# Expert blocks of a two-layer transformer kernel: pairs finished one by one, high terms of the down projection first, weight casts placed around

## The chip, the cores and the metric

The kernel runs on one core of a Trainium2 chip. The metric is the device time of one execution in microseconds; the median of three runs of the kernel before is 967.14 us (966.48 to 967.25). The core has five engines with their own instruction streams: TensorE (matmuls, PE), VectorE (DVE), ScalarE (ACT), GpSimd (POOL) and SyncE (SP, which here only starts transfers). Each engine works through its stream in order and waits on semaphores.

## The reference, cut to what matters

Two layers, each attention and then a mixture of experts, over 2048 tokens of width 256. The change touches the experts alone.

```python
# layer 0: 8 experts, inner width 1024, two per token
hidden = silu(x_flat @ wge.T) * (x_flat @ wue.T)
acc = acc + we[:, None] * (hidden @ wde.T)
# layer 1: 8 experts, inner width 512, two per token, at most 640 rows each
h = einsum('ecd,edf->ecf', exp_batches, W1); inp, gate = split(h, 2, axis=-1)
h = gelu(inp, approximate=False) * gate
exp_out = einsum('eci,eid->ecd', h, W2)
```

## The kernel before, in words

Routing writes every token's row into a table in DRAM, sorted by expert. An expert's rows are cut into blocks of 256 tokens. The last block of an expert whose rows fill at most half of it is a half block: TensorE handles 128 tokens of it, while ScalarE and VectorE still work on tiles for 256. With this data layer 0 has 21 blocks (experts with 4, 3, 2, 3, 1, 3, 3, 2; six are half blocks, each the last of its expert), and layer 1 has 19 (3, 3, 1, 3, 2, 2, 3, 2; six half blocks).

All operands are f16 pairs: a high part and a low part (the value minus the high part). A product is three matmuls: high by high, high by low, low by high. Weights arrive as f32 in a ring of three 1024-column stages (`fetch`, L401, issued by SyncE, which waits until the part that used the stage three parts before has its low part, semaphore `w_ready`). ScalarE casts the high part (`high_part`, L1060, the cast is recorded on L1064), VectorE subtracts to get the low part (`low_part`, L1690, recorded on L1694). An expert of layer 0 has six weight parts (two of gate, up and down each), an expert of layer 1 three. They are placed while another expert computes: layer 0 has two weight slots, so in the first block of expert e the weights of e+1 are placed; layer 1 has four, and the first blocks of experts 0 to 4 place the weights of e+3. `l.beside` (L296) says which parts go behind which pair. The caller passes them as `coming`.

One block, with `pairs` = 4 in layer 0 and 2 in layer 1 (a pair is two 128-wide chunks of the inner width):

- TensorE (`one_block`, L892): for each pair j, 24 matmuls, 12 for gate and 12 for up, into two PSUM banks; two pairs of banks alternate, so pair j waits for the product of pair j-2 (`_h32`). Then eight transposes of the next block's rows (`turn_block`, L884, recorded on L888). Then the down projection: for each chunk c the terms high by high, high by low and low by high for each 128 tokens, chunk pairs waiting on `_h` (the low part of the hidden values); 48 matmuls in a full block of layer 0, 24 in its half block, 24 and 12 in layer 1. It first waits until the previous block's results have left PSUM (`_y`).
- ScalarE (`one_block`, L1184): Silu or Gelu of the gate (L1196), high cast of the product (L1200). In round j it does the activation of pair j and then the high cast of pair j-1, with its weight parts behind the cast (`split`, L1186). After all pairs: the load of the rows of block g+2 (L1182), which waits for `_carried`; then the scaling of the two results by the gate share (L1208, "yb"), which waits for the down projection and for GpSimd's earlier additions; then the last weight parts.
- VectorE (`one_block`, L1696): product with up (L1704, reads PSUM), low subtraction (L1709, both inputs in SBUF). In round j the product of pair j and then the subtraction of pair j-1 and its weight parts. After all pairs `turned` (L1678): copy of the transposed rows (L1680), then the gate shares (L1683 to L1687, `_carried`); then the last weight parts.
- GpSimd (`add_results`, L551): per block two indirect transfers that add the results to the sums (L562). Ahead of the last expert of layer 0 it also scales a table for the next stage (`scale_phi`, L569, recorded on L576).

The order of all this is written out by hand; there is no planner. All matmuls other than transposes are recorded on the helper's line L641.

Of the kernel before, what the change touches and what calls it, by code (L numbers as in the profile page):

```python
# [16 lines left out]
ALU = mybir.AluOpType  # L17
# [5 lines left out]
P = 128  # L23
D = 256
# [46 lines left out]
def two_layers(nc, a, out):  # L71
    with ExitStack() as ctx:
# [206 lines left out]
        for n, l in enumerate(L):  # L279
# [16 lines left out]
            l.beside = (([0], [1], [2], [3], [4, 5]), ([0], [1, 2], []))[n]  # L296
# [342 lines left out]
        def _(pe):  # L639
# [239 lines left out]
            def experts(l):  # L879
# [12 lines left out]
                def one_block(g, wh, wl, width):  # L892
# [17 lines left out]
                    for c in range(l.hc):  # L910
                        if c % 2 == 0:
                            pe.wait_ge(S(r + "_h"), g * pairs + c // 2 + 3)
                        at = l.down_at + c * D
                        for hf in range(width // P):
                            o, tk = ps[:, 4 + hf, 0:D], slice(hf * P, (hf + 1) * P)
                            mm(o, h_hi[:, c, tk], wh[:, at:at + D], c == 0, False)
                            mm(o, h_hi[:, c, tk], wl[:, at:at + D], False, False)
                            last = mm(o, h_lo[:, c, tk], wh[:, at:at + D], False, c == l.hc - 1)
# [125 lines left out]
        def _(act):  # L1044
# [127 lines left out]
            def experts(l):  # L1172
# [11 lines left out]
                def one_block(g, coming=None):  # L1184
# [6 lines left out]
                    for j in range(pairs + 1):  # L1191
                        n = g * pairs + j
                        if j < pairs:
                            act.wait_ge(S(r + "_h32"), n + 1)
                            act.wait_ge(S(r + "_gu_ps"), n * 2 + 1)
                            act.activation(s_act[:, j % 2, :], ps[:, 2 * (j % 2), :], l.act).then_inc(S(r + "_s"), 1)  # L1196
                        if j:

                            act.wait_ge(S(r + "_h32"), n + 2)
                            act.copy(h_hi[:, 2 * j - 2:2 * j, :].rearrange("p c t -> p (c t)"), h32[:, (j - 1) % 2, :]).then_inc(S(r + "_hh"), 1)  # L1200
                            split(j - 1)
                    act.wait_ge(S(r + "_xbT_ps"), g + 3)
                    act.wait_ge(S(r + "_carried"), g + 2)
                    load(g + 2)
                    act.wait_ge(S(r + "_down"), g + 2)
# [5 lines left out]
                    split(pairs)  # L1211
# [103 lines left out]
        def _(dve):  # L1315
# [356 lines left out]
            def experts(l):  # L1672
# [23 lines left out]
                def one_block(g, coming=None):  # L1696

                    for j in range(pairs + 1):
                        n = g * pairs + j
                        if j < pairs:  # L1700
                            dve.wait_ge(S(r + "_s"), n + 1)
                            dve.wait_ge(S(r + "_gu_ps"), n * 2 + 2)
                            dve.wait_ge(S(r + "_h"), n + 1)
                            dve.tensor_tensor(h32[:, j % 2, :], s_act[:, j % 2, :], ps[:, 2 * (j % 2) + 1, :], ALU.mult).then_inc(S(r + "_h32"), 1)  # L1704
                        if j:
                            if j == 1:
                                dve.wait_ge(S(r + "_down"), g + 1)
                            dve.wait_ge(S(r + "_hh"), n)
                            dve.tensor_tensor(h_lo[:, 2 * j - 2:2 * j, :].rearrange("p c t -> p (c t)"), h32[:, (j - 1) % 2, :],  # L1709
                                              h_hi[:, 2 * j - 2:2 * j, :].rearrange("p c t -> p (c t)"), ALU.subtract).then_inc(S(r + "_h"), 1)  # L1710
                            if coming:
                                for c in l.beside[j - 1]:
                                    low_part(*coming, c)
                    turned(g + 1)
                    if coming:
                        for c in l.beside[pairs]:
                            low_part(*coming, c)
# [143 lines left out]
```

## Time and profile before

| what | value |
| --- | --- |
| median of three runs | 967.14 us |
| the profiled execution's own time | 969.82 us |
| its span | 968.1 us |
| mean granted clock of TensorE | 0.861 |
| first expert stage | about 292 to 625 us |
| second expert stage | about 766 to 950 us |

The span is what the profiler records from the first to the last instruction. Times of rows are microseconds from its start. A matmul row's duration is the time of the whole group of matmuls. What stands in square brackets is the idle time of that engine just before the row, and what ended it; "issue" means that nothing in the profile explains it, such as branches and register loads. PEld is TensorE's load of the stationary operand. The names of tiles are those of the arenas: in layer 0 and 1 alike, `keys` holds the product, the transposed rows and the scaled results, `probs` and `slot` hold weights and hidden values, `inbox` the weight stages.

### The profile page before, as it was taken

Reading aid. Unit: us, or ns where it says so; the run is one execution under the profiler, and the core shown is the slowest. Engines: PE = TensorE matmul, PEld = TensorE weight load, DVE = VectorE, ACT = ScalarE, POOL = GpSimd, SP = SyncE. Lnnn points to the kernel's source line nnn. Section 1 sums busy time; section 2 is a strip of 40 time slices with the busy share of each in tenths; the row PEclk is TensorE's granted clock in tenths of the full one; section 3 lists DMA queues with packets and bytes.
Section 4 is the critical chain, followed back from the end, with each engine's and each line's share of the span. In section 5 each row is a group of like instructions: output and inputs, shape, how many; then the busy total and the mean of one; then the engine's idle time right before and its main releaser. Section 6 shows DMA issues by size and latency. Waiting matters only on the chain.

```text
span 968.1 us, 19223 instructions
## 1 busy us (share of the span) xinstructions
PE 742.9 (77%) x6314; PEld 576.9 (60%) x6315; DVE 550.2 (57%) x1363; ACT 402.3 (42%) x720; POOL 324.1 (33%) x319
## 2 busy tenths in 40 slices
PE   5658788897608999999979999978882278778882
PEld 4323545464507888888768788755542266657772
DVE  7786777868454447466456464584537054454441
ACT  1145566766123435445445353443411043444331
POOL 7325002354350221212211213453456323333342
PEclk8788897977658999999989999985555599999997
DMA  4551305114136415255255252142222444452232
GB/s 130 131 118 34 56 0 143 66 40 146 66 123 213 101 34 153 41 155 136 62 152 151 39 153 35 34 163 81 84 75 93 148 105 108 116 117 44 45 60 37
DMA packets 67984, 91.68 MB, mean 95 GB/s; under 512 B 14282, under 2 KB 54019, under 8 KB 67932
## 3 DMA queue, kind: packets, MB, share of 16 engines
q1 hardware_dynamic: 41372, 63.11, 21.7%
q0 software_dynamic: 14592, 16.24, 9.8%
q10 hardware_dynamic: 11968, 11.72, 4.5%
q8 instruction: 24, 0.39, 0.2%
q14 instruction: 28, 0.23, 0.1%
HBM read 63.94 MB, written 29.87 MB: 97 GB/s over the span
## 4 chain that ended last, share of the span: by engine, by line
PE 50%; DVE 21%; issue 14%; ACT 8%; DMA 3%; ACTq 2%; POOL 1%; DVEq 0%; POOLq 0%; SPq 0%
PE ps L641 47%; DVE probs L1709 3%; DVE probs L1624 2%; DVE mx L1489 2%; DVE probs L1694 2%; DVE keys L1704 2%; ACT probs L1124 1%; ACT expo L1121 1%; ACT probs L1196 1%; PE ps L973 1%; DVE keys L1680 1%; DVE slot L1694 1%; DVE stats L1321 1%; ACT probs L1064 1%; ACTq L1181 1%
## 5 line engine op out<-in xcount | busy, mean ns | idle before, releaser
L1704 DVE TENSOR_TENSOR keys<-probs,ps 128x512 f32<-128x512 f32 x122 | 83.2, 687 | 211.0 <-PE ps L641 149.9
L641 PE MATMUL ps<-keys,slot 128*128 128x256 f16 (+1 forms) x1440 | 152.8, 269 | 20.5 <-issue 11.1
L641 PE MATMUL ps<-keys,probs 128*128 128x256 f16 (+1 forms) x1488 | 139.7, 255 | 21.0 <-issue 16.0
L641 PEld LDWEIGHTS ps<-keys,slot 128*128 128x128 f16 x1440 | 130.9, 101 | 41.3 <-issue 21.5
L641 PEld LDWEIGHTS ps<-keys,probs 128*128 128x128 f16 x1488 | 123.7, 98 | 36.0 <-issue 21.4
L562 POOL DMA_INDIRECT attended<-keys,row_to x42 | 69.6, 1656 | 174.5 <-ACT keys L1208 168.1
L1196 ACT ACTIVATE probs<-ps 128x512 f32<-128x512 f32 x122 | 71.9, 598 | 88.6 <-PE ps L641 83.5
L1208 ACT ACTIVATE keys<-ps,carried 128x256 f32<-128x256 f32 x80 | 33.5, 470 | 161.7 <-issue 74.9
L1709 DVE TENSOR_TENSOR probs<-keys,probs 128x512 f16<-128x512 f32 x122 | 87.9, 722 | 3.4 <-ACT probs L1200 1.5
L1200 ACT CAST probs<-keys 128x512 f16<-128x512 f32 x122 | 74.9, 614 | 29.0 <-DVE keys L1704 27.9
L562 POOL DMA_INDIRECT out_x<-keys,row_to x38 | 59.1, 1556 | 70.4 <-ACT keys L1208 64.6
L641 PE MATMUL ps<-slot,probs 128*128 128x256 f16 x636 | 74.0, 273 | 10.0 <-DVE probs L1709 9.8
L1624 DVE TENSOR_TENSOR probs<-expo,probs 128x512 f16<-128x512 f32 x80 | 60.9, 773 | 33.5 <-ACT probs L1124 31.5
L641 PE MATMUL ps<-probs 128*128 128x256 f16 x612 | 72.0, 273 | 10.0 <-DVE probs L1709 9.7
L641 PEld LDWEIGHTS ps<-slot,probs 128*128 128x128 f16 x636 | 60.2, 98 | 20.5 <-DVE probs L1709 13.9
L641 PEld LDWEIGHTS ps<-probs 128*128 128x128 f16 x612 | 57.5, 98 | 21.0 <-DVE probs L1709 14.7
L1121 ACT ACTIVATE expo<-ps 128x512 f32<-128x512 f32 x80 | 48.1, 601 | 52.6 <-PE ps L641 47.0
L558 POOL COPY row_to<-carried 128x2 int32 x40 | 11.1, 277 | 148.4 <-DMA attended<-keys,row_to 53.4
L888 PE MATMUL ps<-identh,probs 128*128 128x128 f16 x336 | 26.5, 223 | 43.1 <-DMA probs<-rows 42.8
L641 PE MATMUL ps<-penalties,identb 128*128 128x462 bf16 x96 | 34.8, 362 | 18.7 <-DVE mx L1489 8.1
L1124 ACT CAST probs<-expo 128x512 f16<-128x512 f32 x80 | 48.9, 618 | 0.0
L888 PEld LDWEIGHTS ps<-identh,probs 128*128 128x128 f16 x336 | 21.8, 100 | 45.4 <-issue 41.7
(256 smaller groups left out, 1243.4 us busy)
## 6 DMA issues: line engine op xcount, KB each, us to landing
inbox<-in_W SPq DMA_DIRECT2D x24, 512.0 KB, 4.0
probs<-rows ACTq DMA_DIRECT2D x44, 260.0 KB
inbox<-in_wg SPq DMA_DIRECT2D x16, 512.0 KB, 4.6
inbox<-in_wu SPq DMA_DIRECT2D x16, 512.0 KB, 3.5
inbox<-in_wd SPq DMA_DIRECT2D x16, 512.0 KB, 3.6
rows<-zeros SPq DMA_DIRECT2D x16, 260.0 KB, 2.1
x<-in_x SPq DMA_DIRECT2D x4, 512.0 KB, 6.3
q_out<-queries SPq DMA_DIRECT2D x8, 256.0 KB, 2.1
```

The lines of the kernel that those rows point to most:

```text
L562: pool.indirect_dma_start(out=l.sums, out_offset=bass.IndirectOffsetOnAxis(ap=row_to[:, hf:hf + 1], axis=0), in_=yb[:, hf, :], in_offset=N ...
L641: return pe.matmul(o, l, r, start=start, stop=stop, **kw)
L888: last = pe.transpose(psh[:, 6, part * BLK + hf * P:part * BLK + (hf + 1) * P], x_raw[:, hf, part * P:(part + 1) * P], identh[:, :])
L1121: act.activation(e_ring[:, u % 4, :], ps[:, 4 + u % 2, :], ACT.Exp, scale=float(DK) ** -0.5).then_inc(S("a0_exp"), 1)
L1124: act.copy(p_hi[:, u - 1, :], e_ring[:, (u - 1) % 4, :]).then_inc(S("a0_phi"), 1)
L1196: act.activation(s_act[:, j % 2, :], ps[:, 2 * (j % 2), :], l.act).then_inc(S(r + "_s"), 1)
L1200: act.copy(h_hi[:, 2 * j - 2:2 * j, :].rearrange("p c t -> p (c t)"), h32[:, (j - 1) % 2, :]).then_inc(S(r + "_hh"), 1)
L1208: ins = act.activation(yb[:, hf, :], ps[:, 4 + hf, 0:D], ACT.Identity, scale=carried[:, bass.ds(g, 1), hf, 0:1].rearrange("p b d -> p (b d)"))
L1624: dve.tensor_tensor(p_lo[:, u, :], e_ring[:, u % 4, :], p_hi[:, u, :], ALU.subtract).then_inc(S("a0_plo"), 1)
L1694: dve.tensor_tensor(w[:, 1, at:at + CH], stage[:, n % STAGES, :], w[:, 0, at:at + CH], ALU.subtract).then_inc(S(f"w_ready{l.n}"), 1)
L1704: dve.tensor_tensor(h32[:, j % 2, :], s_act[:, j % 2, :], ps[:, 2 * (j % 2) + 1, :], ALU.mult).then_inc(S(r + "_h32"), 1)
L1709: dve.tensor_tensor(h_lo[:, 2 * j - 2:2 * j, :].rearrange("p c t -> p (c t)"), h32[:, (j - 1) % 2, :], h_hi[:, 2 * j - 2:2 * j, :].rearran ...
```

## The change

In both `one_block` functions of ScalarE and VectorE the round for pair j now does all of pair j. On ScalarE: activation j, wait for product j, high cast j, weight parts. On VectorE: product j, weight parts (the low ones of the parts behind pair j-1), wait for the high cast, low subtraction j. A second list, `l.low_beside`, gives the low parts their places, one round behind the high ones; in layer 1 the third part moves behind the pairs. ScalarE's last weight parts are cast ahead of the scaling of the results instead of after it. On TensorE the down projection first runs both high terms of all chunks, waiting on the high casts (`_hh`), and then the low terms of all chunks, waiting on `_h`. Numbers and shapes of instructions stay as they are.

```diff
-            l.beside = (([0], [1], [2], [3], [4, 5]), ([0], [1, 2], []))[n]
+            l.beside = (([0], [1], [2], [3], [4, 5]), ([0], [1], [2]))[n]
+            l.low_beside = (([], [0], [1], [2], [3, 4, 5]), ([], [0], [1, 2]))[n]
...
                     for c in range(l.hc):
                         if c % 2 == 0:
-                            pe.wait_ge(S(r + "_h"), g * pairs + c // 2 + 3)
+                            pe.wait_ge(S(r + "_hh"), g * pairs + c // 2 + 1)
...
                             mm(o, h_hi[:, c, tk], wh[:, at:at + D], c == 0, False)
                             mm(o, h_hi[:, c, tk], wl[:, at:at + D], False, False)
+                    for c in range(l.hc):
+                        if c % 2 == 0:
+                            pe.wait_ge(S(r + "_h"), g * pairs + c // 2 + 3)
...
                             last = mm(o, h_lo[:, c, tk], wh[:, at:at + D], False, c == l.hc - 1)
...
+                    for j in range(pairs):
                         n = g * pairs + j
...
+                        act.wait_ge(S(r + "_h32"), n + 1)
+                        act.wait_ge(S(r + "_gu_ps"), n * 2 + 1)
+                        act.activation(s_act[:, j % 2, :], ps[:, 2 * (j % 2), :], l.act).then_inc(S(r + "_s"), 1)
+                        act.wait_ge(S(r + "_h32"), n + 3)
+                        act.copy(h_hi[:, 2 * j:2 * j + 2, :].rearrange("p c t -> p (c t)"), h32[:, j % 2, :]).then_inc(S(r + "_hh"), 1)
+                        split(j)
                     act.wait_ge(S(r + "_xbT_ps"), g + 3)
                     act.wait_ge(S(r + "_carried"), g + 2)
                     load(g + 2)
+                    split(pairs)
                     act.wait_ge(S(r + "_down"), g + 2)
...
                     ins.then_inc(S(r + "_y"), 1)
-                    split(pairs)
...
+                        dve.wait_ge(S(r + "_s"), n + 1)
+                        dve.wait_ge(S(r + "_gu_ps"), n * 2 + 2)
+                        dve.wait_ge(S(r + "_h"), n + 1)
+                        dve.tensor_tensor(h32[:, j % 2, :], s_act[:, j % 2, :], ps[:, 2 * (j % 2) + 1, :], ALU.mult).then_inc(S(r + "_h32"), 1)
+                        if coming:
+                            for c in l.low_beside[j]:
+                                low_part(*coming, c)
+                        if j == 0:
+                            dve.wait_ge(S(r + "_down"), g + 1)
+                        dve.wait_ge(S(r + "_hh"), n + 1)
+                        dve.tensor_tensor(h_lo[:, 2 * j:2 * j + 2, :].rearrange("p c t -> p (c t)"), h32[:, j % 2, :],
+                                          h_hi[:, 2 * j:2 * j + 2, :].rearrange("p c t -> p (c t)"), ALU.subtract).then_inc(S(r + "_h"), 1)
                     turned(g + 1)
                     if coming:
-                        for c in l.beside[pairs]:
+                        for c in l.low_beside[pairs]:
                             low_part(*coming, c)
```

## Rows read from the trace of the kernel before

**Rows 1.** The page, its first part: busy time, share of the span, instructions.
```profile
PE 742.9 (77%) x6314; PEld 576.9 (60%) x6315; DVE 550.2 (57%) x1363; ACT 402.3 (42%) x720; POOL 324.1 (33%) x319
```

**Rows 2.** Waits in one expert stage: engine, line, releaser: us, times, longest.
```profile
PE ps L641 <- DVE keys L1704: 4.0, 6, 0.7
...
PE ps L641 <- DVE probs L1709: 18.2, 23, 1.1
```

**Rows 3.** Timeline, layer 0, a coming block and the next: start, duration, what.
```profile
402.13 10.65 PE L641 MATMUL ps<-keys,slot 128*128 128x256 f16 x96 [2.21 <-issue]
...
404.89 0.60 ACT L1196 ACTIVATE probs<-ps 128x512 f32<-128x512 f32 x1
...
407.27 1.05 ACT L1064 CAST probs<-inbox 128x1024 f16<-128x1024 f32 x1
...
419.53 0.84 ACT L1208 ACTIVATE keys<-ps,carried 128x256 f32<-128x256 f32 x2 [4.43 <-issue]
420.26 1.99 ACT L1064 CAST probs<-inbox 128x1024 f16<-128x1024 f32 x2
...
422.14 1.09 ACT L1196 ACTIVATE probs<-ps 128x512 f32<-128x512 f32 x2
...
424.35 5.41 PE L641 MATMUL ps<-keys,slot 128*128 128x256 f16 x48 [0.65 <-DVE keys L1704]
```

**Rows 4.** Timeline, a half block of layer 0.
```profile
390.89 5.56 PE L641 MATMUL ps<-keys,probs 128*128 128x128 f16 x96
...
392.06 0.60 ACT L1196 ACTIVATE probs<-ps 128x512 f32<-128x512 f32 x1
...
399.08 0.55 PEld L641 LDWEIGHTS ps<-probs 128*128 128x128 f16 x6 [0.22 <-DVE probs L1709]
```

**Rows 5.** Timeline, the change from the one-block expert to the next.
```profile
500.91 2.36 DVE L1694 TENSOR_TENSOR probs<-inbox,probs 128x1024 f16<-128x1024 f32 x2 [3.25 <-ACT probs L1064]
...
504.57 11.95 PE L641 MATMUL ps<-keys,probs 128*128 128x256 f16 x96 [6.54 <-issue]
```

**Rows 6.** Timeline, the scaling on GpSimd and a subtraction beside it.
```profile
603.18 6.52 POOL L576 TENSOR_SCALAR keys<-keys,betas 128x2464 f32<-128x2464 f32 x1
...
604.68 4.85 DVE L1709 TENSOR_TENSOR probs<-keys,probs 128x512 f16<-128x512 f32 x1
```

**Rows 7.** Timeline, a full block of layer 1 and the scaling of its results.
```profile
909.20 5.41 PE L641 MATMUL ps<-keys,probs 128*128 128x256 f16 x48 [1.80 <-issue]
...
916.00 2.79 PE L641 MATMUL ps<-probs 128*128 128x256 f16 x24 [0.94 <-DVE probs L1709]
...
919.32 0.84 ACT L1208 ACTIVATE keys<-ps,carried 128x256 f32<-128x256 f32 x2 [3.34 <-PE ps L641]
```

**Rows 8.** Timeline, a half block of layer 1 and the start behind it.
```profile
928.04 2.84 PE L641 MATMUL ps<-keys,probs 128*128 128x128 f16 x48
...
929.47 0.60 ACT L1196 ACTIVATE probs<-ps 128x512 f32<-128x512 f32 x1
...
930.27 1.46 DVE L1704 TENSOR_TENSOR keys<-probs,ps 128x512 f32<-128x512 f32 x2 [3.01 <-PE ps L641]
...
930.99 0.62 ACT L1200 CAST probs<-keys 128x512 f16<-128x512 f32 x1
...
935.77 5.41 PE L641 MATMUL ps<-keys,probs 128*128 128x256 f16 x48 [1.78 <-issue]
```

**Rows 9.** Timeline, a coming block of layer 1 (start, second pair of down, next block).
```profile
830.08 5.41 PE L641 MATMUL ps<-keys,probs 128*128 128x256 f16 x48 [1.89 <-issue]
...
838.61 1.48 PE L641 MATMUL ps<-probs 128*128 128x256 f16 x12 [0.26 <-DVE probs L1709]
...
841.57 5.41 PE L641 MATMUL ps<-keys,probs 128*128 128x256 f16 x48 [1.47 <-DVE keys L1680]
```

**Rows 10.** TensorE in stretches: busy time (instructions), granted clock, DMA share, GB/s.
```profile
402.00:405.00 3.00, 2.87 (x27) 1.00 0.34 87
480.00:483.00 3.00, 2.88 (x14) 0.50 0.33 86
```

More of the change, by code:

```diff
@@ L917, in one_block @@
                             mm(o, h_hi[:, c, tk], wl[:, at:at + D], False, False)
+                    for c in range(l.hc):
+                        if c % 2 == 0:
+                            pe.wait_ge(S(r + "_h"), g * pairs + c // 2 + 3)
+                        at = l.down_at + c * D
+                        for hf in range(width // P):
+                            o, tk = ps[:, 4 + hf, 0:D], slice(hf * P, (hf + 1) * P)
                             last = mm(o, h_lo[:, c, tk], wh[:, at:at + D], False, c == l.hc - 1)
@@ L1189, in split @@
                                 high_part(l, *coming, n)
-                    for j in range(pairs + 1):
+                    for j in range(pairs):
                         n = g * pairs + j
[L1193 to L1201, printed above, removed]
+                        act.wait_ge(S(r + "_h32"), n + 1)
[4 more added lines that the diff above has]
+                        split(j)
                     act.wait_ge(S(r + "_xbT_ps"), g + 3)
@@ L1696, in one_block @@
                 def one_block(g, coming=None):
-                    for j in range(pairs + 1):
+                    for j in range(pairs):
                         n = g * pairs + j
[L1700 to L1713, printed above, removed]
+                        dve.wait_ge(S(r + "_s"), n + 1)
[10 more added lines that the diff above has]
+                                          h_hi[:, 2 * j:2 * j + 2, :].rearrange("p c t -> p (c t)"), ALU.subtract).then_inc(S(r + "_h"), 1)
                     turned(g + 1)
                     if coming:
-                        for c in l.beside[pairs]:
+                        for c in l.low_beside[pairs]:
                             low_part(*coming, c)
```

## The prediction

> **What bounds the kernel now.** I began with the page. TensorE is busy 77% of the span, VectorE 57%, ScalarE 42% [rows 1]. Both expert stages (about 292 to 625 us and 766 to 950 us, 40 blocks in all) are TensorE streams in which the other engines matter only where a matmul waits. So I listed TensorE's idle pieces in the second stage by releaser: 23 waits on the low subtraction L1709 cost 18.2 us, before the output projection [rows 2]. Then I read single blocks in the timeline. There are three kinds in each layer; T is the start of a block's gate and up matmuls.
>
> First layer (four pairs): a full block runs its 96 gate and up matmuls in 10.65 us, 2.62 a pair, then transposes and down projection, 16.17 us to the next block. The block of an expert on whose side the next expert's weights are placed ("coming" below) runs as long, but its last two weight casts sit on ScalarE behind the scaling of the results (419.53), so the next block's first Silu starts at 422.14 and TensorE loses 0.65 us before pair 2 [rows 3]. Six blocks show this, 0.65 to 0.69 us; such a block takes 17.0 us, a plain one 16.16. A half block (128 tokens, six of them) takes 8.9 us, and 2.2 us of "issue" follow it [rows 3, 4].
>
> Second layer (two pairs): a full block takes 9.43 us with 0.94 of stall before the down projection [rows 7]. A half block takes 7.73 to its successor, with 1.78 of issue in it [rows 8]. A coming block takes 11.49: the same 0.94 before down, then 0.26, then 1.47 behind VectorE, which casts weights ahead of the copy of the next block's tokens [rows 9].
>
> **What the change does to one pair.** Before, ScalarE ran Silu of pair j+1 before the high cast of pair j, so the chains of two pairs overlapped. After, Silu, product and high cast follow one another. Silu start to product start is 0.80 (929.47, 930.27), the product ends 0.69 later, the cast starts 0.03 behind that (930.99) [rows 8], and ScalarE takes its next instruction 0.50 after a 512-wide one: 2.02 us a pair. Beside it a weight cast holds ScalarE 0.95 (1.05 long) [rows 3]: 2.97. A full pair on TensorE is 2.62, a half pair 1.35. So: full plain blocks are untouched, coming blocks drift 0.35 a pair, which the high-terms-first order absorbs, and **half blocks become bound by the chain**. Numbers of matmuls, casts and DMAs don't change.
>
> **First layer, half blocks.** Silu of pair 0 starts at T+1.17 [rows 4]. Silu 3 then starts at T+1.17+3x2.02 = 7.23, high cast 3 ends at 7.23+0.80+0.69+0.03+0.61 = 9.36. TensorE has done everything up to there and still has 4 high and 8 low matmuls at 0.109: end T+10.8 against 8.9 now (+1.9). The 2.2 us of issue: in every half block the last wait (399.08) is 2.7 to 3.1 us before the next start (402.13) and 0.66 of matmuls lie in it [rows 3, 4], while after a full last block almost none shows. I take it that the sequencer's work runs beside matmuls issued after the last wait. After the change twelve instead of six follow, which hides 0.65 more. Five blocks x 1.22, and the last one, behind which no expert waits, 1.9: **+8.0 us**. Bounds: +1.9 each without that cover (+11.4), 0 if ScalarE's order cost nothing.
>
> **First layer, blocks after coming ones.** Weight parts 4 and 5 are now cast before the scaling. Part 5 is fetched after low part 2, about 1 us later than now, the yb scaling comes about 1.2 to 2.7 us later, but Silu 0 of the next block directly behind it. Product 0 is then ready about 0.5 to 0.7 us before pair 2 wants it: 17.0 becomes 16.16, 6 x -0.84 = -5.0; expert 2, whose Silu 0 is held to T+2.76 by a table load [rows 3], gives 0.2 back at its own last high cast: **-4.8 us**. Bound: 0 if part 5 lands later.
>
> **One-block expert.** TensorE waits 6.54 us at 504.57 for the weight parts whose last low cast ends at 503.27, behind yb [rows 5]. Casts ahead of yb end about 501.9: **-1.3 us** (0 to -1.6).
>
> **The scaling of phi on GpSimd.** It takes 6.52 us from 603.18, and the subtraction L1709 that meets it lasts 4.85 instead of 0.69 [rows 6]; the product, which reads PSUM, isn't held. Now the held subtraction has only subtractions behind it at first. In the new order the next pair's product waits behind it: if subtraction 1 is caught (T+6.9, phi starts near T+6.6 to 7.2), high cast 3 ends near T+16.4 and the block 1.5 us later than now; if subtraction 2 is, nothing changes. I take **+0.8**.
> The Trainium skill (SBUF — State Buffer, "Who interferes with whom") says the pair of ports shared by VectorE and GpSimd is an exclusive lock, and that a tensor_tensor with both inputs in SBUF contends with GpSimd's reads. The trace agrees, 4.85 against 0.69; by that rule alone the term would be the same two ends, 0 or +1.5.
>
> **Second layer, coming blocks** (five). High cast 0 ends T+4.2; Silu 1 moves from T+4.14 to T+5.0 behind the weight cast, high cast 1 ends T+7.1. Down high terms of pair 0 run T+5.7 to 6.6, pair 1's from 7.2, low terms to T+9.0, and the token copy no longer waits for two weight parts (done T+8.8). 11.49 becomes about 9.1; for the five -2.5, -2.5, -1.4, -2.1, -2.5 with what precedes them: **-11.0 us**.
> **Full plain blocks.** High terms start 0.94 earlier, 0.28 is lost at high cast 1 (ends T+6.79): 9.43 becomes 8.60. But load and yb hang on VectorE's side, which doesn't move: 919.32 is T+10.12 [rows 7], now 1.5 into the next block instead of 0.7. After a coming block yb is later still and Silu 0 with it, so those three gain nothing, and the one that ends expert 4 loses 1.0 at the change of expert: 4 x -0.8 + 0.2 + 1.0 = **-2.0 us**.
> **Half blocks** (six). Silu 0 goes from T+1.42 to 2.21 behind the late yb, Silu 1 to T+4.23, high cast 1 ends T+6.36, low subtraction 1 T+7.15, next start +2.8: 10.0 instead of 8.0. 5 x 2.0 + 1.6 = **+11.6 us**. Bounds: +0.7 each if yb isn't late, +2.5 if row loads land later.
> Further, ScalarE has 0.8 us of branches after yb at the entry of experts 3 and 4, hidden now; I take **+1.0** for them and for row loads that arrive with weights.
>
> **Sum.** +8.0 -4.8 -1.3 +0.8 = +2.7 in the first layer, -11.0 -2.0 +11.6 +1.0 = -0.4 in the second: +2.3, less 0.2 for rounding: +2.1 us. The profiled execution took 969.82 us around a span of 968.1; the same difference applied to the median of the runs, 967.14, gives 969.2.
>
> **Rivals.**
> (a) Faster: yb isn't late in the second layer, because what lies between VectorE's "carried" and the scaling (1.44 us, load included) shrinks when TensorE is already done. For it: after half blocks the gap is partly GpSimd's. Against: it is the same 1.44 in every undisturbed block. Six half blocks save 0.8 each and 1 us elsewhere: -3.7, 965.5 to 963. It decides from a lag under 0.7 us.
> (b) Slower by clock: TensorE's granted clock was 0.50 at 480 to 483 us, after a half block and 2.2 us of idleness, and 1.00 at 402 to 405 after an equal one [rows 10]; the 96 matmuls took 12.2 us against 10.65, so one low start costs 1.6. Half blocks now stand idle 1.6 us more inside. If three to four more starts fall to 1.2 GHz: +5 to +6, 974.5.
> The Trainium skill (TensorE: Matmul & The Clock Gate, "Part 1: The HAM clock gate") says that the throttled state is the default and activity releases it. The rows at 480 us agree; by it more idleness only raises the chance of (b).
> (c) No change: the terms cancel within 0.2%, 967.1. It is the near half of the forecast's own spread.
>
> **Chances.** The forecast's case 0.55, by itself 966.5 to 971.5, of which 0.25 lies within 0.2% (1.9 us, what a measurement here can tell from nothing) and 0.30 above; (a) 0.25, of which 0.05 is within; (b) 0.20. Faster 0.20, same 0.30, slower 0.50. Range 963.5 to 975.0.
>
> **What would show it.** The first layer's half blocks: Silu starts 2.0 us apart, down projection ending near T+10.8. Blocks after coming ones without the 0.65 us wait. The second layer's full blocks 8.6 apart, its half blocks 10.0, coming ones 9 to 10.5. Waits of TensorE turn from L1709 to the high cast. Wrong would be: half blocks at their old lengths, coming blocks with TensorE waiting for products, or many changed clocks at block starts.

## The result, and the profile after

The changed kernel takes 987.3 us (median of four runs, 985.2 to 993.2) against 967.0: 1.0226 times as long [1.0191, 1.0261], 20 us more. The forecast was 969.2 with a range to 975.0: the direction was right, the size was a tenth of what came. The profiled execution took 993.15 us around a span of 991.4, so against the span of 968.1 before it is 23.3 us longer.

The page, first part and TensorE's clock:

```profile
span 991.4 us, 19242 instructions
PE 758.3 (76%) x6314; PEld 584.4 (59%) x6315; DVE 555.3 (56%) x1363; ACT 404.3 (41%) x720; POOL 317.8 (32%) x319
...
PEclk9789898886659999999989999975555599889886
```

The numbers of instructions are those of [rows 1]. TensorE is busy 15 us longer with the same matmuls, so some of them ran at the lower clock; the rest of the 23 us is idleness. Its waits in the second expert stage (784 to 970 us; engine, line, releaser: us, times, longest) answer to [rows 2]:

```profile
PE ps L642 <- issue: 12.5, 8, 2.6
PE ps L642 <- ACT probs L1204: 10.1, 16, 1.4
PE ps L889 <- DMA probs<-rows: 4.1, 5, 0.9
PE ps L642 <- DVE slot L1698: 1.6, 1, 1.6
PE ps L642 <- DVE probs L1698: 1.5, 1, 1.5
```

The 18.2 us behind the low subtraction are gone; 10.1 behind the high cast, 4.1 behind row loads and 3.1 behind VectorE's low parts of weights stand in their place. Read block by block, from one block's first gate matmul to the next one's, the two profiled executions compare so (us; the last column is how much of the difference lies between the start and the end of the gate and up matmuls, that is in the low clock or in waits for products; what a full block's gate and up take beyond their time at 2.4 GHz is called the excess below):

| stretch | before | after | difference | of it gate and up time |
| --- | --- | --- | --- | --- |
| layer 0, first block | 18.7 | 21.6 | +2.9 | +2.9 |
| layer 0, 5 half blocks | 55.6 | 66.6 | +11.0 | +3.6 |
| layer 0, 6 blocks behind coming ones | 102.4 | 97.4 | -5.0 | -5.0 |
| layer 0, other 8 blocks | 142.0 | 143.7 | +1.7 | +2.3 |
| last half block and the way to layer 1 | 154.8 | 160.4 | +5.7 | +0.6 |
| layer 1, 5 coming blocks | 61.9 | 58.6 | -3.3 | +5.0 |
| layer 1, 8 full blocks | 75.5 | 73.5 | -1.9 | +4.1 |
| layer 1, 5 half blocks | 39.5 | 50.0 | +10.5 | 0 |
| before the first block, behind the last start | 317.8 | 319.5 | +1.7 | |

Three of these rows vary on their own. In the eighteen profiles of this case the way to the first block took 284.7 to 299.0 us, the first block 18.5 to 22.9, and the last half block with the way to layer 1 152.8 to 160.4, though the code ahead of the first block and between the layers is nearly the same in all. In the first block of the change 2.62 us of issue stand where before 0.30 did.

A half block of layer 0, TensorE, ScalarE and VectorE, beside [rows 4] (T is 396.77; start, duration, what, in brackets the idle time before it and its releaser):

```profile
396.77 4.22 PE L642 MATMUL ps<-keys,probs 128*128 128x128 f16 x72
...
397.94 0.60 ACT L1202 ACTIVATE probs<-ps 128x512 f32<-128x512 f32 x1
...
399.99 0.59 ACT L1202 ACTIVATE probs<-ps 128x512 f32<-128x512 f32 x1
...
401.53 1.51 PE L642 MATMUL ps<-keys,probs 128*128 128x128 f16 x24 [0.53 <-DVE keys L1707]
402.03 0.59 ACT L1202 ACTIVATE probs<-ps 128x512 f32<-128x512 f32 x1
...
404.07 0.59 ACT L1202 ACTIVATE probs<-ps 128x512 f32<-128x512 f32 x1
...
405.57 0.62 ACT L1204 CAST probs<-keys 128x512 f16<-128x512 f32 x1 [0.92 <-DVE keys L1707]
406.23 0.69 DVE L1714 TENSOR_TENSOR probs<-keys,probs 128x512 f16<-128x512 f32 x1 [0.68 <-ACT probs L1204]
...
406.25 1.49 PE L642 MATMUL ps<-probs 128*128 128x256 f16 x12 [1.42 <-ACT probs L1204]
...
409.99 2.22 PE L642 MATMUL ps<-keys,slot 128*128 128x256 f16 x11 [2.26 <-issue]
```

These rows show the chain: Silus 2.04 apart, the last high cast 1.5 behind the last Silu, TensorE idle 0.53 for a product and 1.42 for the cast, and the down projection ending at T+10.97. The 2.26 us of issue behind it are as long as the 2.21 of [rows 3].

Layer 1, TensorE alone: a full block, a half block and a start behind it, beside [rows 7 to 9]:

```profile
826.10 5.41 PE L642 MATMUL ps<-keys,slot 128*128 128x256 f16 x48 [0.48 <-issue]
...
832.99 1.92 PE L642 MATMUL ps<-slot,probs 128*128 128x256 f16 x16 [0.16 <-ACT probs L1204]
834.75 2.84 PE L642 MATMUL ps<-keys,slot 128*128 128x128 f16 x48
838.41 0.62 PE L889 MATMUL ps<-identh,probs 128*128 128x128 f16 x8 [0.82 <-DMA probs<-rows]
839.28 0.60 PE L642 MATMUL ps<-slot,probs 128*128 128x256 f16 x4 [0.25 <-ACT probs L1204]
841.23 1.12 PE L642 MATMUL ps<-slot,probs 128*128 128x256 f16 x8 [1.36 <-ACT probs L1204]
844.71 8.30 PE L642 MATMUL ps<-keys,probs 128*128 128x256 f16 x48 [2.36 <-issue]
...
857.96 2.24 PE L642 MATMUL ps<-keys,probs 128*128 128x256 f16 x19 [1.59 <-DVE slot L1698]
```

The full block takes 8.65 (9.43 before), the half block 9.96 (7.85), and the 48 matmuls behind it 8.30 us where those of [rows 9] took 5.41. The stretches say why (us, busy time of each engine, granted clock, DMA share, GB/s; the second row is of the kernel before, the same place of its block):

```profile
844.80:848.00 3.20, 3.20 (x16) 2.27 (x17) 0.00 (x0) 1.06 (x3) 1.56 (x1) 0.50 0.40 88
```
```profile
830.20:833.50 3.30, 3.30 (x32) 2.96 (x31) 0.59 (x1) 1.44 (x3) 1.50 (x2) 1.00 0.33 86
```

Half as many matmuls in the same time: 1.2 GHz. All five starts behind layer 1's half blocks are above 5.41 us like this one (7.08, 8.30, 7.88, 8.12, 6.81 us); before, one was (7.08).

### The profile page after: what moved, and what is told of

It reads as the page before. It is cut to its first block, busy times and chain, and to the rows that moved or that the text cites. A ratio compares the mean times of both kernels' runs of the same rounds, so it can differ in the third digit from the quotient of the medians.

```text
span 991.4 us, 19242 instructions
## 1 busy us (share of the span) xinstructions
PE 758.3 (76%) x6314; PEld 584.4 (59%) x6315; DVE 555.3 (56%) x1363; ACT 404.3 (41%) x720; POOL 317.8 (32%) x319
## 4 chain that ended last, share of the span: by engine, by line
PE 49%; DVE 19%; issue 14%; ACT 10%; ACTq 2%; DMA 2%; POOL 1%; another core or an unknown queue 1%; DVEq 1%; POOLq 0%; SPq 0%
PE ps L642 45%; DVE keys L1707 4%; ACT probs L1202 3%; DVE probs L1628 2%; DVE mx L1493 2%; ACT probs L1204 2%; DVE keys L1684 1%; ACT probs L1131 1%; PE ps L980 1%; ACT expo L1128 1%; DVE stats L1325 1%; PE ps L889 1%; ACTq L1188 1%; DMA probs<-rows 1%
## 5 line engine op out<-in xcount | busy, mean ns | idle before, releaser
L642 PE MATMUL ps<-keys,slot 128*128 128x256 f16 (+1 forms) x1440 | 155.5, 272 | 21.0 <-issue 15.4
L642 PE MATMUL ps<-keys,probs 128*128 128x256 f16 (+1 forms) x1488 | 149.1, 264 | 20.7 <-issue 16.9
L642 PEld LDWEIGHTS ps<-keys,probs 128*128 128x128 f16 x1488 | 128.3, 101 | 40.9 <-issue 21.5
L563 POOL DMA_INDIRECT attended<-keys,row_to x42 | 65.4, 1558 | 201.7 <-ACT keys L1213 195.3
L642 PE MATMUL ps<-probs 128*128 128x256 f16 x612 | 74.4, 277 | 13.6 <-ACT probs L1204 13.1
L642 PEld LDWEIGHTS ps<-slot,probs 128*128 128x128 f16 x636 | 59.8, 98 | 20.6 <-ACT probs L1204 12.3
L559 POOL COPY row_to<-carried 128x2 int32 x40 | 8.8, 221 | 139.7 <-DMA attended<-keys,row_to 45.0
```

Source lines behind the costliest of these rows:

```text
L563: pool.indirect_dma_start(out=l.sums, out_offset=bass.IndirectOffsetOnAxis(ap=row_to[:, hf:hf + 1], axis=0), in_=yb[:, hf, :], in_offset=N ...
L642: return pe.matmul(o, l, r, start=start, stop=stop, **kw)
```

## The experiments

Sixteen kernels ran, each beside the kernel before on the same chip; that one's median was 968.1 to 969.8 us there and 967.0 beside the change, so kernels are compared by their ratios to it, turned into us by 967. Each has one profiled execution. The theory after the result (A): the loss is the pair-by-pair order in half blocks, where a chain of 2 us a pair meets 1.35 us of TensorE work, and the low clock behind the longer idle time. Rivals: (B) the weight casts ahead of the scaling of the results; (C) the new order of the down projection.

**One part at a time.** e1_order is the kernel before with the TensorE part of the diff alone (the second loop over the chunks). e2_chain has ScalarE's and VectorE's rounds alone, with the down projection and the weight places as before. e3_parts has the places alone:

```diff
-            l.beside = (([0], [1], [2], [3], [4, 5]), ([0], [1, 2], []))[n]
+            l.beside = (([0], [1], [2], [3], [4, 5]), ([0], [1], [2]))[n]
+            l.low_beside = (([0], [1], [2], [], [3, 4, 5]), ([0], [], [1, 2]))[n]
...
                     load(g + 2)
+                    split(pairs)
                     act.wait_ge(S(r + "_down"), g + 2)
...
-                    split(pairs)
```

and e4_order_parts is e1 and e3 together: the whole change without the pair-by-pair rounds.

> The kernel before with one part of the change: the down projection runs all high terms first (waiting on the high casts), then the low terms. ScalarE and VectorE keep their old order and places. Theory A (the loss of the change comes from finishing pair by pair, above all in half blocks, and from a lower clock at block starts): this part alone is a gain, full blocks of the second layer 9.43 -> about 8.75, its half blocks -0.5, first layer unchanged: -8 us, about 959. Theory B (the weight casts ahead of the scaling of the results cause the loss): also a gain here. Theory C (the new order of the down projection itself costs, by its extra waits or by more low-clock time): slower than before.

> The kernel before with one part of the change: ScalarE and VectorE finish each pair before the next. Order of the down projection and places of the weight casts as before. Theory A: half blocks of the first layer last 10.9 instead of 8.9 us to the end of down (six of them, +11.5), half blocks of the second layer +1.5 each (+9), full blocks the same, and more low-clock starts (+0 to +8): 985 to 995. Theory B: within 3 us of before. Theory C: within 3 us of before.

> The kernel before with one part of the change: the last weight parts are cast ahead of the scaling of the results, the low parts after the copy of the next rows, and in the second layer the third part behind the pairs. Pair order and down projection as before. Theory A: a gain: six blocks of the first layer 17.0 -> 16.16, the change after the one-block expert -1.3, five blocks of the second layer -1.4 each: -12 us, about 955. Theory B: slower than before, by 5 to 15 us, with TensorE waiting on the low parts at changes of expert and on late scaled results.

> The whole change without the pair-by-pair order: high terms first and the new places of the weight parts, ScalarE and VectorE still overlapping pairs. Theory A: the two gains add or more (coming blocks of the second layer reach about 9): -20 to -24 us, 943 to 947. Theory B: slower than before. Theory C: slower than the run with the weight places alone.

| kernel | us (median, range) | against before | half block in its profile, mean of five, layer 0 / layer 1 |
| --- | --- | --- | --- |
| before | 969.8 (967.0 to 972.4) | 1 | 11.1 / 7.9 |
| e1_order | 977.6 (976.5 to 978.7) | 1.0094 [1.0068, 1.0120] | 11.4 / 8.6 |
| e2_chain | 1017.9 (1016.3 to 1021.6) | 1.0516 [1.0480, 1.0552] | 13.1 / 9.7 |
| e3_parts | 958.8 (957.1 to 961.3) | 0.9890 [0.9862, 0.9918] | 11.1 / 7.9 |
| e4_order_parts | 962.7 (961.9 to 966.3) | 0.9942 [0.9913, 0.9972] | 11.3 / 8.6 |
| the change | 987.3 (985.2 to 993.2) | 1.0226 [1.0191, 1.0261] | 13.3 / 10.0 |

(B) fell: the weight places are worth 11 us by themselves, from six blocks of 16.17 instead of 17.0 us and coming blocks of layer 1 of 9.9 to 10.9 instead of 11.5 to 11.8 (at full clock). The pair-by-pair order costs 50 us alone, far more than (A) said; its profile has TensorE waiting 1.20 us in a half block for the low part of the last pair, on which the old down projection hangs. The ten half blocks with a start behind them hold 19 of the 47 us by which its profiled execution is longer; the rest is spread over coming blocks, low starts and the stretch between the layers, and wasn't taken apart. (C) was half right: high terms first was to gain 8 us and lost 9. In e1's layer 1 full blocks at full clock do take 8.60 us, but the half blocks take 0.7 us more, and seven starts are at the low clock where before two were. Summed over layer 1, the eight full blocks get 5.9 us shorter by the order and 8.1 longer by the clock, and the five half blocks get 3.5 longer. The profile of e1, TensorE, shows both in one place:

```profile
904.95 2.84 PE L641 MATMUL ps<-keys,slot 128*128 128x128 f16 x48
908.72 0.62 PE L888 MATMUL ps<-identh,probs 128*128 128x128 f16 x8 [0.93 <-DMA probs<-rows]
909.61 1.74 PE L641 MATMUL ps<-slot,probs 128*128 128x256 f16 x12 [0.26 <-ACT probs L1206]
913.58 7.02 PE L641 MATMUL ps<-keys,probs 128*128 128x256 f16 x48 [2.24 <-issue]
```

The full block ahead ended 0.8 us sooner, but the row load (it hangs on VectorE's `carried`) didn't, and the half block waits 0.93 us for it.

**Is it the idle time, through the clock?** e5_fill_stall puts matmuls with an unused result into the wait for the last cast, 12 in layer 0 and 10 in layer 1; e6_fill_both has 18 more behind the down projection.

```diff
+                        if width == P and c == l.hc - 2:
+                            for _ in range((12, 10)[l.n]):
+                                mm(ps[:, 7, 0:D], identh[:, :], wh[:, 0:D], True, True)
                         if c % 2 == 0:
                             pe.wait_ge(S(r + "_hh"), g * pairs + c // 2 + 1)
...
                     last.then_inc(S(r + "_down"), 1)
+                    if width == P:
+                        for _ in range(18):
+                            mm(ps[:, 7, 0:D], identh[:, :], wh[:, 0:D], True, True)
```

> The changed kernel, with 12 (layer 0) or 10 (layer 1) extra matmuls of 256 columns in each half block, ahead of the last pair's high terms, that is in the 1.4 us in which TensorE waits for ScalarE's cast; their result goes to an unused PSUM bank. Chain theory (the loss is the 2 us more that each half block takes, by dependence): the lengths of half blocks stay at 13.2 and 9.9 us and the time stays at 984 to 990. Clock theory (part of the loss is that this idle piece brings the clock down to the lower level in the next block's gate and up): layer 1's starts go back from 7.5 to 8.3 us to about 5.5 us in most of the six blocks, and the time falls by 5 to 11 us, to 976 to 982.

> As the run before, and 18 more matmuls of 256 columns (about 1.9 us) behind the output projection of each half block, where TensorE shows an idle piece of 2.2 to 2.6 us put down to issue. If that piece runs beside matmuls that are already issued, the half blocks keep their length and, by the clock theory, the starts behind them are all at the full clock: 974 to 980. If it only begins when the matmuls are through, each of the 12 half blocks gets 1.9 us longer, and the time is 995 to 1010. The chain theory alone gives 984 to 990 in the first case.

e5 took 988.4 us (985.7 to 992.6), 1.0212 [1.0163, 1.0262]: no change, although in its profile three of the five starts behind layer 1's half blocks were back at 5.41 us. That run can't be told from the change, so filling the inner wait alone shows no gain. e6, on the same chip, took 984.3 (982.8 to 986.8), 1.0161 [1.0114, 1.0209]. In its profile all five of those starts are at 5.41 and three in layer 0 are at 10.65 instead of 12.1 to 12.3:

```profile
840.83 2.13 PE L642 MATMUL ps<-slot,identh 128*128 128x256 f16 x18
843.55 5.41 PE L642 MATMUL ps<-keys,probs 128*128 128x256 f16 x48 [0.60 <-issue]
```

The excess of gate and up time fell from 6.8 to 2.7 us in layer 0 (its first block left out) and from 13.2 to 1.5 in layer 1: 15.8 us less, while the half blocks got 0.6 us longer in layer 0 and 0.25 in layer 1, 5 in all if all twelve did. All four executions of e6 have a granted clock of 0.876 to 0.879, those of e5 0.854 to 0.858 and those of the change 0.844 to 0.853 (the kernel before: 0.860 to 0.880), so the clock did come back. In time, e6's ratio is 6 us under the change's, but the two intervals overlap, so a gain isn't shown by the times. The kernel before had 4.5 and 4.1 us of the same excess itself (the waits for products left out), so in the profiled executions the clock makes 11.4 us of the loss in the expert blocks, 2.3 in layer 0 and 9.1 in layer 1: a part of it.

**Is it the chain in half blocks?** e13_halves_old keeps the change but runs ScalarE's and VectorE's rounds in the overlapped order in half blocks. e7_narrow keeps the pair-by-pair order but works on the 128 columns that a half block uses; e14_before_narrow is the same edit on the kernel before. On ScalarE (VectorE has the same), with `w` choosing the rounds in the one and the width in the others:

```diff
+                    half = act.value_load(tb[0:1, bass.ds(e + TB_PACKED, 1)], min_val=0, max_val=PACK * 2 * PACK) % 2
+                    def either(g):
+                        with act.If(g + half >= end):
+                            one_block(g, w=P)
+                        with act.If(g + half < end):
+                            one_block(g)
```

> The changed kernel, with ScalarE's and VectorE's five operations per pair on 128 columns of each chunk instead of 256 in half blocks (the other half of the columns is never read there). Chain theory: the Silu, product, cast and difference of a pair become about half as long, TensorE no longer waits for the last pair, and the half blocks go back from 13.2 to about 11 us in layer 0 and from 9.9 to about 7.6 to 8 us in layer 1: 12 times 2 us, less some branches on ScalarE and VectorE, 960 to 970. Clock theory: the stall goes too, so the starts behind go back to the full clock, 952 to 962. If the cost was elsewhere (order of the output projection alone, row loads), half blocks stay above 12 and 9 us and the time above 978.

> The whole change, but ScalarE and VectorE use the overlapped order of before in half blocks (all at full width). If the pair-by-pair chain in half blocks is the loss, half blocks go from 13.2 to about 11.3 us and from 10.0 to about 8.6 us (lengths of the run without the pair-by-pair order), 5 times 1.9 and 5 times 1.4 us and two more of the last ones, and with two to three low starts fewer the time is 962 to 972. If the chain's cost lay in other blocks or in the clock alone, it stays above 978.

> The kernel before, with ScalarE and VectorE on 128 columns per chunk in half blocks. If narrow work helps only by breaking the pair-by-pair chain, 966 to 972. If it helps in any order (half blocks of layer 0 from 11.1 to about 10.3 us, those of layer 1 from 7.9 to about 7.3), 12 times 0.7 us, less 1 to 2 us of branches: 958 to 964.

e13 took 967.5 us (960.9 to 970.4), 0.9978 [0.9947, 1.0009]: with half blocks in the old order the loss of 22 us is gone, 24 us less. Its profile has half blocks of 11.4 and 8.66 us (six times 1.9 and six times 1.3 less, 19 us) and 5.5 us less excess in layer 1's gate and up time. The rest of the profile is less neat: the stretch between the layers took 5.7 us less, and layer 1's first block 4.3 more, with 3.7 us of waits for high casts ahead of and in its down projection (0.5 in the change). Its half block of layer 0, TensorE:

```profile
391.33 5.66 PE L642 MATMUL ps<-keys,probs 128*128 128x128 f16 x96
396.83 0.61 PE L889 MATMUL ps<-identh,probs 128*128 128x128 f16 x8
397.28 3.06 PE L642 MATMUL ps<-probs 128*128 128x256 f16 x24
...
402.61 1.67 PE L642 MATMUL ps<-keys,slot 128*128 128x256 f16 x7 [2.27 <-issue]
```

e7 took 963.0 (959.1 to 964.4), 0.9932 [0.9903, 0.9960], 28 us less than the change. e14 took 962.0 (955.8 to 965.7), 0.9931 [0.9902, 0.9960], 7 less than before. So of e7's 28 us some 7 are what narrow work gives in either order, and 21 come from breaking the chain, near e13's 24. These gains hold some clock too. In e7 all five starts behind layer 1's half blocks are still low, but at 6.7 to 7.1 us, and its excess is 2.2 us in layer 0 and 8.8 in layer 1, 9 less than the change's 6.8 and 13.2; e13's is 8.7 and 7.8, 4 less. So most of both gains isn't clock.

**What sets a half block's length.** In these profiles I read when the last low subtraction ends (T is the block's start) and how much later the next block starts. Before, the second half block of layer 0 (T is 390.89, the next start 402.13) has it here:

```profile
397.57 1.46 DVE L1709 TENSOR_TENSOR probs<-keys,probs 128x512 f16<-128x512 f32 x2
```

Its end is T+8.14; in the change the row at 406.23 above ends at T+10.15. The table gives the second half block of layer 0 and the third of layer 1; the third and fourth of layer 0 agree with the second within 0.03 us:

| kernel | layer 0: subtraction ends | next start behind it | layer 1: ends | next start |
| --- | --- | --- | --- | --- |
| before | T+8.14 | 3.10 | T+5.07 | 3.13 |
| the change | T+10.15 | 3.07 | T+7.17 | 3.09 |
| e4_order_parts | T+8.14 | 3.09 | T+5.83 | 3.08 |
| e13_halves_old | T+8.19 | 3.09 | T+5.83 | 3.09 |
| e7_narrow | T+7.23 | 3.08 | T+5.57 | 3.08 |
| e14_before_narrow | T+7.22 | 3.09 | T+4.20 | 3.10 |
| e6_fill_both | T+10.15 | 3.70 | T+7.17 | 3.34 |

But for e6, the subtraction's end moves by 3 us and the distance behind it by 0.06. In the code, the wait for that subtraction is TensorE's last in the block; behind it come two to six matmuls and then the branches and register loads of the change of expert. By these rows 3.1 us pass (2.6 to 2.9 at the other changes of expert in the table's kernels, e6 aside) from there to the first matmul of the next expert, whether TensorE still has 0.8 us of matmuls to run (the change) or 1.4 (e7). What makes up the 3.1 us the profiles don't show. More matmuls fit beside it: e6's 18, some 2.0 us of work, made it 0.61 and 0.25 us longer. The first half block of layer 0 is apart: 2.85 to 2.88 in the kernels with the old down projection (before, e3, e14), 3.8 to 4.2 in the change, e4, e7 and e13, which have the new one, but 2.85 again in e5, which has the new one with 12 matmuls more in its middle; why, no run tells.

The Trainium skill (TensorE: Matmul & The Clock Gate, "Architectural detail: the array is 16× 32×32, not 1× 128×128") gives TensorE a queue of 64 instructions. In the change only two matmuls of 0.11 us lie behind the last wait and 0.82 us of work is left at its release, so the sequencer was ahead of its matmuls, which agrees; no run here shows the depth.

**The shares ahead of the copy.** VectorE works out the gate shares (`carried`), on which the row load hangs, right behind its last product instead of after the copy of the turned rows. e8_shares is this on the change, e9 on e4, e11 on e3, e10 is e9 with narrow work, e12 is e11 with 12 matmuls behind the down projection.

```diff
                         dve.tensor_tensor(h32[:, j % 2, :], s_act[:, j % 2, :], ps[:, 2 * (j % 2) + 1, :], ALU.mult).then_inc(S(r + "_h32"), 1)
+                        if j == pairs - 1:
+                            shares(g + 1)
```

> The changed kernel, with VectorE working out the next block's gate shares right behind its last product instead of after the copy of the turned rows, so that the row load that waits for them is issued about 1.6 us earlier. If the row load sets when the next block's transposes can start in layer 1, the waits of 0.8 to 0.9 us ahead of the transposes go; in half blocks the stall on the last cast is then longer by the same amount, and the lengths stay: 984 to 989. If the late rows are a cost of their own, 12 to 20 blocks of layer 1 get 0.3 to 0.8 us shorter: 975 to 983.

> The whole change but the pair-by-pair order (as in the order-and-parts run, 962.7), with the gate shares worked out ahead of the copy of the turned rows. If the row loads hold what high terms first should give in layer 1 (waits of 0.5 to 1.0 us ahead of the transposes of half blocks), half blocks of layer 1 go from 8.6 to about 7.9 us: 957 to 961. If high terms first costs through longer idle pieces and the lower clock behind them, the starts in layer 1 stay at about 7 us of gate and up in four to five blocks, and the time stays within 1 us of 962.7.

> As the run before, with ScalarE and VectorE on 128 columns per chunk in half blocks. In the overlapped order the pair takes TensorE as long as ScalarE (1.39 us) in half blocks of layer 0, and its last cast sets the end: half blocks of layer 0 would go from 11.3 to about 10.3 us (five times) and those of layer 1 by 0.3 to 0.5 us: 7 us less than the run before, less 1 to 2 us of branches: 951 to 957. If TensorE and the issue behind the blocks set their length already, it is within 1 us of the run before.

> The weight places alone (958.8), with the gate shares ahead of the copy of the turned rows. In layer 1 the subtraction of the last pair, for which the down projection waits in this order, moves 0.5 to 1 us back, and the row loads come 1.6 us earlier. If late rows cost nothing in this order, 958 to 964; if they do, 953 to 957.

> As the run before, with 12 extra matmuls of 256 columns behind the down projection of each half block, into an unused PSUM bank. If the issue piece behind half blocks runs beside matmuls that are already issued (18 of them made the block 0.63 us longer and not 1.95), 12 cost 0.1 to 0.4 us a block; and if idleness there brings the clock down, the starts behind half blocks at 7.1 and 12.3 us go to 5.4 and 10.65. Clock theory: 3 to 5 such starts at 1.7 us less 12 times 0.3 us: 1 to 5 us less than the run before. Without it: 1 to 5 us more.

e8 took 982.3 us (975.1 to 983.7), 1.0139 [1.0093, 1.0185], 8 less than the change: layer 1's half blocks no longer wait for rows and go from 10.0 to 8.9, 5 us for the five. (Its profiled execution is its fastest, with the first block 10 us earlier than in the change's, so the two can't be compared as wholes.) e9 took 973.2 (968.6 to 977.0), 1.0041 [1.0013, 1.0069], and e11 977.4 (971.5 to 982.4), 1.0089 [1.0047, 1.0130]: 10 and 19 more than without the edit, outside every expectation. TensorE in a full block of e11's layer 1 waits 1.51 instead of the 0.94 of [rows 7]:

```profile
911.71 5.41 PE L642 MATMUL ps<-keys,probs 128*128 128x256 f16 x48 [2.04 <-issue]
...
918.32 1.29 DVE L1715 TENSOR_TENSOR probs<-keys,probs 128x512 f16<-128x512 f32 x2
919.07 2.79 PE L642 MATMUL ps<-probs 128*128 128x256 f16 x24 [1.51 <-DVE probs L1715]
```

In the pair-by-pair order VectorE waits for the cast at that point and the shares cost nothing; in the overlapped order they push back both last subtractions. Half blocks show it too (8.5 instead of 7.9). e10 took 958.7 (953.9 to 964.9), 0.9896 [0.9822, 0.9970]. e12 took 975.6 (972.0 to 978.0), 1.0069 [1.0041, 1.0097]: its profile has one low start in each layer where e11's has three, and its interval overlaps e11's, so a gain isn't shown.

**The better versions.** Narrow half blocks on e3 and on e4:

> The weight places alone (958.8) with narrow work in half blocks: the gain of the run before on top of it: 950 to 956 if narrowness helps in any order, 957 to 962 if not.

> Weight places and high terms first (962.7) with narrow work in half blocks. High terms first takes 0.8 us from each full block of layer 1 (8.6 for 9.43), and costs low starts. If narrow work shortens the half blocks' idle pieces, the starts behind them keep the full clock and the gain of the order shows: 946 to 953. If the starts stay low, 952 to 958, about the run before.

e15 took 948.8 us (947.7 to 950.5), 0.9809 [0.9777, 0.9841]; e16 945.8 (944.1 to 950.8), 0.9791 [0.9746, 0.9836]. Both are 2% under the kernel before and 4% under the change; which of them is ahead can't be told. e16's layer 1 has full blocks of 8.60 us, half blocks of 7.6 (e15: 9.42 and 7.0) and two low starts in its 13 full-width blocks, as e15 has, and takes 165.0 us from its first start to its last against 167.5: high terms first is worth 2.5 us there, where 8 were expected of it. In layer 0 and on the way to layer 1 e16 is 2.6 us behind. Its profiled span is 4 us shorter because its first block starts 5 us earlier, ahead of all that the two kernels do differently.

## Why the prediction was wrong, point by point

- *Chain of a pair, 2.02 us; down projection ending at T+10.8; waits turning to the high cast.* Right: 2.04, T+10.97 by the row, and the waits above.
- *Layer 0's half blocks +8.0: +1.9 each, less 0.65 hidden in the issue behind.* This step failed. The last wait of a half block isn't for the high cast but, as before, for the last low subtraction, which the new order moves by the full 2.01 us (T+8.14 to T+10.15), and 3.1 us follow in either kernel. At that release 0.8 us of matmuls are left, before it was 0.9, so nothing more is hidden. +2.0 each came, just over the upper bound of 1.9, and the first one took 1.0 more in a longer issue: +11.0 for the five with a start behind them, and 1.8 in the sixth.
- *Blocks behind coming ones, 17.0 to 16.16, -4.8.* Right: -5.0.
- *One-block expert -1.3.* Its wait went from 6.54 [rows 5] to 5.26 us. Right.
- *phi +0.8.* The second of its two cases came: the subtraction of pair 2 was held for 4.57 us, and the block took 0.34 more. The Trainium skill's rule (SBUF — State Buffer, "Who interferes with whom"), that a tensor_tensor with both inputs in SBUF contends with GpSimd's reads, is borne out once more: 4.57 us against 0.69.
- *Layer 1: coming blocks -11.0, full ones -2.0, half ones +11.6.* Without the clock they were -8.3 (-3.3 less 5.0), -6.0 (-1.9 less 4.1: blocks behind a coming one gain 0.8 too, which the forecast denied) and +10.5 for five of the six half blocks: -3.8 to the last start, where the forecast has -2.0 (its -0.4 without the 1.6 of the last half block). With the clock it is +5.3.
- *The clock, rival (b), "three to four more starts, +5 to +6", chance 0.20.* In layer 1 four more starts fell, for +9.1 us, not 1.6 each: a start cost 1.4 to 2.9. Layer 0 had 2.3 us more, and in the stretch between the layers the first 16 matmuls on `queries` took 8.90 us instead of 7.54. It should have been part of the forecast, which itself saw that half blocks stand idle 1.6 us longer ahead of their issue. The Trainium skill (TensorE: Matmul & The Clock Gate, "HAM oscillation — how this bites in real kernels") describes a kernel whose waits bring back the low clock each time round. The five of five low starts here agree, and in e6, with the idle pieces filled, none of the five is low; e4, whose pieces behind the half blocks are as long but which waits less inside, has three of five.
- *Rival (a), faster because the scaling isn't late,* fell: the first Gelu of a half block starts at T+2.24 to T+2.37 in five of six and at T+2.54 in the last (2.21 forecast), and rows came late on top of it, by 0.76 to 0.93 us.

So two steps failed: the cover behind the half blocks, and the clock, which the forecast's sum put at nothing and left to a rival with one chance in five. The profiled executions differ by 21 us more than the forecast's +2.1. Of these the clock in the expert blocks is 11.4, and the half blocks of layer 0 are 4.8 (+12.8 against +8.0). The first block (+2.9) and the way to layer 1 without its half block (+3.8) are most of the rest, and both vary between profiles by as much. By the runs' medians the 22 us come out as: pair-by-pair rounds in half blocks +24 (e13, low starts behind them included), the same rounds elsewhere with their places of low parts +3 (e13 against e4, whose intervals overlap), weight places -11 (e3), high terms first +5 on top of these (e4 against e3: the intervals just overlap, the runs on the same chip don't, 961.9 to 966.3 against 957.1 to 961.3; +9 alone in e1). High terms first should have gained; the late rows and the clock in layer 1 took it back. Open stays the stretch between the layers, which took 152.8 to 160.4 us between profiles though its code, the last half block aside, is nearly the same.

## What to carry to other kernels

Where a block ends in a change of loop, find the sequencer's last wait. Here its release, and not the end of the matmuls, set the next start: with 0.4 to 1.4 us of matmuls still to run at that moment the distance was the same. Weigh an order of a chain against the shortest block that goes through it: rounds one by one cost nothing in plain blocks of 2.6 us a pair and 2 us a block in those of 1.35. A helper engine that works on half-empty tiles is on the path exactly there, so cutting its work to the columns in use was worth 0.7 to 2.9% in each of the five kernels that got it (the change, before, e3, e4, e9).

## What the runs showed of the hardware

- From the end of the subtraction that TensorE's last wait is for to the first matmul behind the loop's end took 3.07 to 3.11 us in 48 half blocks (the second to fourth of layer 0 in all sixteen kernels without matmuls added behind them), whenever it came.
- A gain can come back as clock: e1 took 0.8 us out of each full block, but seven starts instead of two were at 1.2 GHz, and the kernel was 9 us slower with less waiting ahead of the down projections of its full blocks. In the change a low start behind a half block of layer 1 cost 1.4 to 2.9 us on top of 5.41.
- Eighteen matmuls without use, 2 us of work, cost 0.61 us a block of layer 0 where they ran beside the branches, and twelve cost 0.09 (e12 beside e11). With the eighteen the granted clock of the whole execution was 0.876 to 0.879 (e6), without them 0.854 to 0.858 (e5).
